# A flag raised and read earlier, and weights centred once in place of centring in three norms, in a fused attention and feed-forward kernel

## The reference

```python
x = x + layernorm(attn(layernorm(x), Wq, Wk, Wv, pre_proj, post_proj, mem_k, mem_v, Wo, bo))
x = x + layernorm(ffn(layernorm(x), w_gate, w_up, w_down))

# attn: 16 heads of 64, 16 memory keys in front of the 512 keys
dots = einsum('bhid,bhjd->bhij', q, k) * scale
dots = einsum('bhij,hk->bkij', dots, pre_proj)      # heads mixed
dots = where(causal, neg, dots)
vk = top_k(dots, 64)[..., -1:]                      # the 64th largest of each row
attn = softmax(where(dots < vk, neg, dots))
attn = einsum('bhij,hk->bkij', attn, post_proj)     # heads mixed again
out = einsum('bhij,bhjd->bhid', attn, v) @ Wo + bo

# ffn: h = silu(x @ wg.T) * (x @ wu.T); out = h @ wd.T, weights int / 127
# layernorm(x) = (x - mean(x)) / sqrt(var(x) + 1e-5), over the 128 features, no gain or bias
```

## Time and profile before

| | |
|---|---|
| median of 3 runs | 3648.22 us (3642.02 to 3651.94) |
| profiled execution, own time | 3646.99 us |
| its span | 3645.2 us |
| granted TensorE clock, mean | 0.88 |
| busy: PE, VectorE, ScalarE, GpSimd | 77%, 81%, 86%, 56% |
| first score tile taken | at 105 us |
| DMA | 22.66 MB, 1.9% of 16 engines |

### The profile page before, as it was taken

How to read it: one execution, slowest core, us unless ns; L and a number is a source line. 1 busy time by engine, 2 the same in 40 slices (tenths; PEclk the granted TensorE clock), 3 DMA queues, 4 the chain that set the end, 5 groups by cost and what they waited for, 6 DMA issues and landing times. The chain is left out here.

```text
span 3645.2 us, 70387 instructions
## 1 busy us (share of the span) xinstructions
PE 2805.3 (77%) x13751; PEld 1832.9 (50%) x13751; DVE 2939.2 (81%) x12540; ACT 3139.1 (86%) x8666; POOL 2034.0 (56%) x3767
## 2 busy tenths in 40 slices
PE   7777778787767777777787767877778887777765
PEld 3454555555445555555555545555455554555543
DVE  4588888888888888888888878888888888888884
ACT  1799899898978989899898978989899998989972
POOL 4345556555655555565655546655565665555544
PEclk9889888888888989899898988889898888989877
DMA  1000000000000000000000000000000000000000
GB/s 41 7 2 2 5 8 5 8 2 5 8 4 8 2 10 2 5 8 5 8 2 11 2 4 8 5 8 2 4 8 5 8 2 10 2 5 8 2 7 4
DMA packets 31404, 22.66 MB, mean 6 GB/s; under 512 B 3201, under 2 KB 30338, under 8 KB 30722
## 3 DMA queue, kind: packets, MB, share of 16 engines
q1 hardware_dynamic: 30722, 16.03, 1.5%
HBM read 11.83 MB, written 4.19 MB: 4 GB/s over the span
## 5 line engine op out<-in xcount | busy, mean ns | idle before, releaser
L897 ACT ACTIVATE signs<-scores,state 128x528 int8<-128x528 f32 (+3 forms) x3072 | 1763.6, 574 | 97.5 <-DVE state L1106 21.7
L1301 POOL TENSOR_SCALAR probs<-probs,rinv 128x528 f32<-128x528 f32 (+3 forms) x1024 | 539.3, 545 | 1415.0 <-DVE rinv L1159 1413.6
L766 PE MATMUL t_bank<-ident,probs 128*128 128x128 f32 x2560 | 524.2, 353 | 730.0 <-POOL probs L1301 710.2
L1309 POOL TENSOR_TENSOR work<-scores,work 128x528 f32<-128x528 f32 (+3 forms) x1024 | 887.8, 899 | 13.1 <-DVE work L1038 13.1
L766 PEld LDWEIGHTS t_bank<-ident,probs 128*128 128x128 f32 x2560 | 348.9, 173 | 1025.6 <-issue 854.2
L742 PE MATMUL s_bank<-xn,gT 128*128 128x512 f32 (+3 forms) x2048 | 814.4, 509 | 6.2 <-ACT gT L828 4.0
L1154 DVE SCALAR_TENSOR_TENSOR probs<-scores,kth,expo 128x528 f32<-128x528 f32 (+3 forms) x1024 | 534.2, 577 | 258.9 <-issue 256.1
L753 PEld LDWEIGHTS y_bank<-u_all,probsT 128*128 128x128 f32 x5120 | 626.2, 197 | 108.0 <-issue 100.0
L753 PE MATMUL y_bank<-u_all,probsT 128*128 128x128 f32 x5120 | 635.1, 281 | 6.0 <-ACT probsT L908 6.0
L908 ACT COPY probsT<-t_bank 128x512 f32<-128x512 f32 (+1 forms) x768 | 399.8, 521 | 267.2 <-PE t_bank L766 264.8
L897 ACT ACTIVATION_READ_ACCUMULATOR signs<-scores,state 128x1 f32 x3072 | 579.4, 189 | 0.0
(11 more groups left out here) (144 smaller groups left out, 3089.7 us busy)
## 6 DMA issues: line engine op xcount, KB each, us to landing
xwork<-in_L_attn_x_dram SPq DMA_DIRECT2D x17, 256.0 KB, 2.7
xres<-in_L_attn_x_dram SPq DMA_DIRECT2D x16, 256.0 KB, 2.9
out_dram<-ybuf SPq DMA_DIRECT2D x16, 256.0 KB, 2.4
u_all<-in_L_attn_Wq_dram SPq DMA_DIRECT2D x1, 512.0 KB, 3.8
u_all<-in_L_attn_Wk_dram SPq DMA_DIRECT2D x1, 512.0 KB, 4.6
u_all<-in_L_attn_Wv_dram SPq DMA_DIRECT2D x1, 512.0 KB, 5.4
u_all<-in_L_attn_Wo_dram SPq DMA_DIRECT2D x1, 512.0 KB
expo<-in_L_ffn_w_gate_dram SPq DMA_DIRECT2D x1, 192.0 KB, 4.8
```

What stands on the lines that cost most here:

```text
L766: mm = nc.tensor.transpose(t_bank[q % 2][:, at:at + P], probs[:, h % 2, KEY_AT[t] + j * P:KEY_AT[t] + (j + 1) * P], ident[:, :])
L897: nc.scalar.activation(signs[:, k, 0:ROW[t]], row(scores, ring(head_of(s, k + 1), RING), t), ACT.Sign, bias=guesses(s % STATES, k, GUESSES ...
L1301: nc.gpsimd.tensor_scalar(prb, prb, rinv[:, slot_p, t:t + 1], 1.0, ALU.mult, ALU.mult).then_inc(scaled, 1)
L1309: nc.gpsimd.tensor_tensor(wrk, row(scores, slot_k, t), wrk, ALU.subtract).then_inc(hidden, 1)
```

## The change

**Flag.** PE raises the flag at the start of a step, ahead of all four score tiles, once VectorE has taken the last step's scores (`masked`), and waits for VectorE's copy only in front of the last score tile. VectorE copies the flag ahead of the guess update in place of after it, and no longer waits for the scores there. It loads the register right behind the first count, ahead of the feed-forward's gate instructions; two more counts stand between that and the branch; the fourth stays behind the probabilities.

**Centring.** In the prologue Wo, the bias and the gate and up weights lose the mean of each row (`centre_rows`: a sum, then an update with two inputs), and the down weights are turned with a centred identity (`centre`). What Y, X1 and Z are made of is thus centred. For Y, X1 and Z GpSimd multiplies by `rstd` alone, in one instruction of 512 elements; for x it subtracts the mean and multiplies, in two. `ln_out` counts 1 a norm in place of 4.

```diff
@@ PE, prologue
-                    pe.wait_ge(ffn_w_ready, 3)
+                    pe.wait_ge(ffn_w_ready, 5)
...
+                    if i == len(turns) - 1:
+                        mm = nc.tensor.matmul(dst, lhsT=src, rhs=centre[:, :], start=True, stop=True)
+                    else:
+                        mm = nc.tensor.transpose(dst, src, ident[:, :])
...
+            pe.wait_ge(wo_centred, 2)
...
+            pe.wait_ge(bias_centred, 2)
@@ PE, score
                     if t == SCORE_ORDER[-1] and lagged(kind, s, LAG_P):
-                        raise_flag(s, g - LAG_P)
+                        pe.wait_ge(flag_taken, g - LAG_P + 1)
@@ PE, step
+                    if lagged(kind, s, LAG_P):
+                        at_least(pe, masked, 4 * H * B if kind == "drain" else 4 * g)
+                        raise_flag(s, g - LAG_P)
                     if kind != "drain":
                         score(kind, b, par, s, g)
-                    elif lagged(kind, s, LAG_P):
-                        pe.wait_ge(masked, 4 * H * B)
-                        raise_flag(s, g - LAG_P)
@@ VectorE, prologue
+            dve.wait_ge(ident_made, 2)
+            nc.vector.tensor_scalar(centre[:, :], ident[:, :], -1.0 / P, None, ALU.add).then_inc(centre_made, 1)
...
+            def centre_rows(rows, sums, n, done):
+
+                nc.vector.tensor_reduce(sums, rows, AX_X, ALU.add).then_inc(done, 1)
+                dve.wait_ge(done, n + 1)
+                nc.vector.scalar_tensor_tensor(out=rows, in0=sums.unsqueeze(2).to_broadcast(list(rows.shape)),
+                                               scalar=-1.0 / D, in1=rows, op0=ALU.mult, op1=ALU.add).then_inc(done, 1)
+
+            centre_rows(wo_s[:, :, :], wo_sum[:, :], 0, wo_centred)
+            centre_rows(bias[:, :].rearrange("p (a d) -> p a d", a=1), bias_sum[:, :], 0, bias_centred)
             dve.wait_ge(w_in, 16 * 10)
             for a in range(3):
                 nc.vector.tensor_scalar(w_f[:, a], w_int[:, a], 1.0 / 127.0, None, ALU.mult).then_inc(ffn_w_ready, 1)
+            dve.wait_ge(ffn_w_ready, 2)
+            centre_rows(w_f[:, 0:2].rearrange("p a c n -> p (a c) n"), row_sum[:, :], 3, ffn_w_ready)
@@ VectorE, step: behind the checks, ahead of the guess update
+                    if applies:
+                        dve.wait_ge(flag_full, gp + 1)
+                        alone(dve)
+                        v.tensor_copy(flags[:, :], flag_part).then_inc(flag_taken, 1)
@@ VectorE, step: behind the guess update
-                    if applies:
-                        dve.wait_ge(flag_full, gp + 1)
-                        if kind != "drain":
-                            dve.wait_ge(scores_full, 4 * g + 4)
-                        alone(dve)
-                        v.tensor_copy(flags[:, :], flag_part).then_inc(flag_taken, 1)
@@ VectorE, step: behind count_found(ORDER[0])
+                    if applies:
+                        dve.wait_ge(flag_taken, gp + 1)
+                        alone(dve)
+                        rows_missed = dve.value_load(flags[0:1, T:T + 1].bitcast(I32), min_val=0, max_val=2 ** 31 - 1)
@@ VectorE, step: behind the gates
+                    if selects:
+                        count_found(ORDER[1])
+                        count_found(ORDER[2])
+
                     if applies:
-                        dve.wait_ge(flag_taken, gp + 1)
-                        alone(dve)
-                        rows_missed = dve.value_load(flags[0:1, T:T + 1].bitcast(I32), min_val=0, max_val=2 ** 31 - 1)
                         at_least(dve, t_full, 3 * (gp - 1))
@@ VectorE, step: behind the probabilities
                     if selects:
-                        for t in ORDER[1:]:
-                            count_found(t)
+                        count_found(ORDER[3])
@@ GpSimd, norm
-                for t in range(T):
-                    nc.gpsimd.tensor_scalar(dst[:, t, :], src[:, t, :], meanvar[:, t, 0:1], rstd[:, t:t + 1], ALU.subtract,
-                                            ALU.mult).then_inc(ln_out, 1)
+                if what == "x":
+                    nc.gpsimd.tensor_tensor(dst[:, :, :], src[:, :, :], meanvar[:, :, 0:1].to_broadcast([P, T, D]),
+                                            ALU.subtract).then_inc(ln_centred, 1)
+                    pool.wait_ge(ln_centred, 1 if kind == "pro" else b + 2)
+                    alone(pool)
+                    src = dst
+                nc.gpsimd.tensor_tensor(dst[:, :, :], src[:, :, :], rstd[:, :].unsqueeze(2).to_broadcast([P, T, D]),
+                                        ALU.mult).then_inc(ln_out, 1)
@@ GpSimd, prologue
+            pool.wait_ge(wo_centred, 2)
             mix_wo(0)
```

More of the change, by code:

```diff
@@ L452, in build @@
         ln_rstd = sem("ln_rstd")
+        ln_centred = sem("ln_centred")
         ln_out = sem("ln_out")
@@ L607, in turn_x @@
             def turn_x(kind, b, par):
-                pe.wait_ge(ln_out, 4 * ln_index(kind, b, "x") + 4)
+                pe.wait_ge(ln_out, ln_index(kind, b, "x") + 1)
                 share(kind, b, ("XT",))
@@ L685, in make_extra @@
                 if use[0] == "X1T":
-                    pe.wait_ge(ln_out, 4 * ln_index(kind, b, "X1") + 4)
+                    pe.wait_ge(ln_out, ln_index(kind, b, "X1") + 1)
                 if use == ("GATE", 0):
```

14 lines of the change are left out of this document (11 added, 3 removed).

## The result

The changed kernel takes **3555.59 us** (median of 4 runs, 3552.53 to 3560.93), against 3646.08 of the kernel before (4 runs): ratio 0.9752, 95% interval 0.9732 to 0.9772, 90.5 us less. I had forecast 46 less. The profiled execution took 3553.21 us, its span 3551.4 against 3645.2: 93.8 less.

A forecast was written before the change was run, and what follows sets the result against it. VectorE's work plus its stalls set a step, with ScalarE next to limit. 15 batches at -2.75 us (-41), the first -5, prologue +5, end -5.5: -46 us, 3602 as a median, range 3545 to 3655.

The forecast's parts named there:

- Branch: VectorE, before the probabilities: two counts issued ahead cover load and branch, gaining 0.87 us a step of 0.99 idle.
- Light steps: Steps 2 to 7, 10 and 14: ScalarE can't pass about 12.15 us, so each gains 0.3, -2.4 a batch.
- Gate steps: Steps 11 to 13: VectorE has 1.4 us more work, ScalarE waits, so each gains 0.6, -1.8 a batch.
- step 0: First step of a batch: gains VectorE's whole 0.65 us.
- step 8: VectorE waits for PE here; ScalarE, further behind, delays PE's transposes: +0.9 us, between -1.5 and +2.5.
- Steps 1, 9, 15: GpSimd's new norm multiply holds VectorE's last guess-update instruction, +0.9 us each; with longer L1309 overlap +1.2 a batch.
- Rival (a): The GpSimd multiply misses or doesn't hold the last guess instruction; steps 1, 8, 9, 15 regain 0.9 each: 3548, chance 0.22.
- Flag copy: VectorE, copy moved ahead of the guess update: net +0.2 us a step, the 42.1 us of flag waits mostly gone.
- Prologue: VectorE's added sums and subtractions take 4.9 us, partly offset by PE's shorter wait: +5 us, 0 to 8.
- End: Behind the last step three norms lie on the chain, each 1.27 against 3.14 us: -5.5 us.
- (b): Slower: the flag wait, now ahead of the guess update, binds in light steps and steps 8 and 9: 3700, chance 0.10.
- (c): Slower: the branch's refill waits for an empty engine, so it isn't covered: near 3700, half of that 3650; chance 0.08.

The follow-up runs named there:

- waiting norms: The changed kernel with GpSimd's norm instructions of steps 1, 8, 9 and 15 waiting for the end of the guess update: 3549.91 us, ratio 0.9711.
- centring alone: The changed kernel with flag, count and branch edits undone, leaving centred weights and one-instruction norms: 3668.15 us, ratio 1.0055 against the kernel before.
- the change without the counts: The changed kernel with its second and third count behind the probabilities again: 3614.26 us, ratio 0.9909 against the kernel before.
- flag alone: The kernel before with early flag product, copy and register load, other three counts behind the probabilities, no centring: 3594.94 us, ratio 0.9864.
- late copy: The changed kernel with VectorE's flag copy behind the guess update again, the product still early on PE: 3555.19 us, ratio 0.9744.

## Why the prediction was wrong

- **Branch:** right in kind. Idle 256.1 to 11.7 us. But VectorE's step is only 0.3 shorter, for a reason that I did not give. Of the 0.99 in the light step above, 0.16 comes back ahead of the count and some 0.65 as longer L1078, L1090 and L1095 (0.25, 0.25 and 0.15; what the copy took behind L1106 makes up for the rest), since GpSimd's L1347 now runs 1 us further into VectorE's next step (to 3.6 in place of 2.6 us).
- **Light steps -2.4 a batch:** -2.1, the right number by luck. That ScalarE limits them was right, but its 12.15 us was read from a stretch cut at VectorE's step ends and is too low: a light head costs it 12.5, before and after. VectorE's light steps average 12.6 and 12.3 us, so by this limit only 0.1 a step was to be had. The rest of the -2.1 is VectorE running ahead; the batch got shorter where ScalarE waits for PE.
- **Gate steps, step 0, step 8:** -2.0, -0.5 and +1.3, near the terms. Step 8 is the place, as I had it, but a term is missing. The copy waits there for PE, and the guess update, late by that, runs into GpSimd's residual sum. Its first instruction is held to 1.26 in place of 0.17:

```profile
1430.27 0.15 DVE L1102 COPY flags<-s_bank 1x5 f32<-1x5 f32 x1 [2.61 <-PE s_bank L746]
1430.50 1.26 DVE L1113 TENSOR_TENSOR state<-counts,consts 128x12 f32<-128x12 f32 x1
...
1430.46 1.27 POOL L1267 TENSOR_TENSOR xres<-xres,ybuf 128x512 f32<-128x512 f32 x1
```

Added up over the eleven instructions of the update, against the median of each, step 8 loses 1.1 us on average in this way; L1139 alone shows 0.1 of it. The waiting norms take it all away, and step 8 gets only 0.2 shorter (16.5 to 16.3): the copy's wait grows by 0.4 there.

- **Steps 1, 9, 15, +1.2 a batch: the step that failed.** I wrote that "both chains start at L1055, so this should repeat in each of the four". The steps got 1.1 us a batch shorter: by VectorE's steps these 2.3 us a batch are 34 of the 44 us by which I missed. The hold itself was right: it appears in all of them in centring alone (0.95) and in the change without the counts (0.87), where the multiply's 1.04 us, not 1.27, make it 0.7 to 0.8 longer and not 0.9. But the counts push the probabilities 1 us towards the step's end, and with them GpSimd's scaling and L1347. GpSimd then comes to its norm from its own queue, late: the multiply starts near 6.2 to 6.3 us of VectorE's step, not at 5.8. L1139 moved to about 6.2 too, so margins of 0.2 us either way decide: over the loop's 14 batches it is held in 5 in step 9, in 8 in step 15, in step 1 never. I had seen the longer L1309 (+0.4) and charged VectorE for it, but not GpSimd's own next work. Nor was the price right where the hold came: taking it away in all four steps gave 12 us, since the waits behind it took the rest. Rival (a), at 3548, was the near one, by its "multiply misses"; but it gives back 0.9 in step 8, too, which the sum had not charged to the hold. Without that it says 3561.
- **Flag copy +0.2 and its place:** the place is indifferent. The flag's worth, 50 us alone, was in the early load beside the gates, the product ahead of the scores, and the first batch; I did not price the three apart. There the old copy waited for the scores in step 6; before, then after:

```profile
158.92 0.15 DVE L1113 COPY flags<-s_bank 1x5 f32<-1x5 f32 x1 [3.54 <-PE s_bank L744]
```

```profile
150.50 0.15 DVE L1102 COPY flags<-s_bank 1x5 f32<-1x5 f32 x1
```

- **Prologue +5:** +0.3 in this execution. Over all profiled executions the first step ends at 107.5 to 110.8 us with centring and 107.3 to 108.8 without, so 5 was too much. The terms were too small all the same: the six instructions take 10.7 us, not 4.9, since GpSimd's L1272 holds two of them, the bias's update (128 elements) and that of the feed-forward weights (3.39). Most of the time lies beside other work.

```profile
17.59 3.71 DVE L981 SCALAR_TENSOR_TENSOR bias<-bias_sum,bias 1x128 f32<-1x128 f32 x1
...
17.55 8.03 POOL L1272 TENSOR_TENSOR scores<-u_all,expo 128x2048 f32<-128x2048 f32 x2 [15.23 <-DVE u_all L981]
```

- **End -5.5:** -7.8. Each multiply takes 1.04, not the 1.27 of L1230, against 3.14 for the four pieces:

```profile
3546.21 1.05 POOL ybuf L1261
```

- **Rivals (b) and (c):** neither came. The flag wait lies mostly in step 8 (30 of 37.9 us in all), and no refill of the branch was left.

## What to carry to other kernels

When a change moves a paced engine's work within its step, follow it through the queue of every engine behind it before forecasting that two instructions will meet: here 1 us of shift on VectorE became 0.4 on GpSimd's norm and turned a sure collision into one that comes in some batches. A stall removed pays only up to the next wait: 46 us of held instructions gave 12 back, since two of four steps then waited for PE. A step of one engine is not the period of the loop: look for the engine that has no idle time from one head to the next, and ask what is left of its waits. And parts of one change should be priced in pairs: the centring costs 17 to 20 us alone or with the flag, and gives 16 with counts and flag.

## What the runs showed of the hardware

- A GpSimd TENSOR_TENSOR of 512 elements held a VectorE TENSOR_TENSOR of 12 elements (0.17 us) where it had started first, so that the latter took up to 1.27 us (step 8 of the late copy, beside the residual sum). Beside the multiply the held one ends 0.02 to 0.03 us behind the multiply (1499.29 and 1499.26; 1475.13 and 1475.10; 1447.24 and 1447.22), so it was let go some 0.15 before the multiply's end, if it takes its 0.17 once free. It did not touch the one-input counts (0.76).
- A piece of the old TENSOR_SCALAR norm held the same instruction far less. Started 0.02 us behind it, in the kernel before, it held nothing (0.17 to 0.20), nor did a last piece hold L1154 in the earlier trace rows. Started 0.14 ahead, in flag alone, with some 0.65 us still to run, it made the 0.17 us 0.32 (the row below merges two pieces):

```profile
1255.02 0.32 DVE L1111 TENSOR_TENSOR state<-state,move 128x12 f32<-128x12 f32 x1
...
1254.88 1.58 POOL L1225 TENSOR_SCALAR xwork<-xres,meanvar,rstd 128x128 f32<-128x128 f32 x2 [0.18 <-POOL rstd L1221]
```

The Trainium skill (SBUF — State Buffer, "SBUF: two separate sides") has an exclusive lock for the whole instruction, taken by whichever starts first, for any GpSimd operation that reads SBUF against a VectorE operation with two SBUF inputs. The TENSOR_TENSOR rows agree but for the last 0.15 us, this TENSOR_SCALAR row does not.
- A broadcast second input made GpSimd's TENSOR_TENSOR no slower: 1.04 us for the multiply, against 1.27 for the residual sum with two full inputs of the same size.
- The idle time behind the branch (some 0.6 us) vanishes but for some 0.1 us where counts already issued are still running.
